# Attention with 77 keys: the softmax's exponentials taken head by head from the score bank, with bias and accumulated sum

## What is computed

```python
def _L0_xattn_ref(x, context, Wq, Wk, Wv, Wo, bo):
    scale = DIM_HEAD ** (-0.5)
    q = (x @ Wq).reshape(B, S, HEADS, DIM_HEAD).transpose(0, 2, 1, 3)
    k = (context @ Wk).reshape(B, L, HEADS, DIM_HEAD).transpose(0, 2, 1, 3)
    v = (context @ Wv).reshape(B, L, HEADS, DIM_HEAD).transpose(0, 2, 1, 3)
    attn = jnp.einsum('bhsd,bhld->bhsl', q, k) * scale
    attn = jax.nn.softmax(attn, axis=-1)
    out = jnp.einsum('bhsl,bhld->bhsd', attn, v)
    out = out.transpose(0, 2, 1, 3).reshape(B, S, INNER)
    return out @ Wo + bo

x = x + _L0_xattn_ref(_layernorm(x, axis=-1), ctx_768, ...)
x = x + _L0_ffn_ref(_layernorm(x, axis=-1), ...)
```

## Time and profile before

| | |
|---|---|
| median of 3 runs | 553.39 us (549.96 to 554.64) |
| the profiled execution | 549.97 us, its span 548.1 us |
| PE busy | 531.5 us, 97% of the span |
| DVE busy | 473.7 us, 86% |
| ACT busy | 294.8 us, 54% |
| POOL busy | 231.3 us, 42% |

### The profile page before, as it was taken

One profiled execution on the slowest core, in us unless ns is written; L12 is line 12 of the kernel. 1 busy time (PEld: TensorE's weight loads), 2 busy tenths in 40 slices (PEclk: granted clock), 3 DMA queues, 4 the chain that ended last, 5 costly groups with the idle time before them and its releaser, 6 DMA issues.

```text
span 548.1 us, 8031 instructions
## 1 busy us (share of the span) xinstructions
PE 531.5 (97%) x2704; PEld 357.9 (65%) x2704; DVE 473.7 (86%) x876; ACT 294.8 (54%) x414; POOL 231.3 (42%) x349
## 2 busy tenths in 40 slices
PE   8989889999999999999998799999999999999997
PEld 8868678887888878788777544444444445544444
DVE  4966888989989899898988599999999988899884
ACT  4834646556555654554443555555545533999500
POOL 4386749679596886856544000000000000055442
PEclk9999999999999999999999899999999999999999
DMA  8718365756668565435969917750442220399987
GB/s 310 277 45 304 104 187 180 249 181 192 209 206 252 171 224 185 154 101 182 202 99 329 269 33 293 273 145 24 117 115 46 70 39 15 121 327 229 149 107 129
DMA packets 82658, 93.82 MB, mean 171 GB/s; under 512 B 46801, under 2 KB 49873, under 8 KB 82361
## 3 DMA queue, kind: packets, MB, share of 16 engines
q1 hardware_dynamic: 77593, 84.13, 49.8%
q0 software_dynamic: 4320, 7.87, 9.6%
q10 hardware_dynamic: 704, 1.31, 0.8%
HBM read 47.51 MB, written 37.78 MB: 156 GB/s over the span
## 4 chain that ended last, share of the span: by engine, by line
PE 78%; DVE 11%; SPq 4%; DMA 2%; issue 2%; ACT 1%; POOL 0%; DVEq 0%; POOLq 0%
PE QO L1133 14%; PE SP L1133 14%; PE QO L193 5%; PE QO L195 5%; PE QO L194 5%; PE SP L464 4%; PE PTP L1240 3%; PE QO L1240 3%; PE SP L1240 3%; SPq L41 2%; SPq L37 2%; PE MI L584 2%; PE MI L583 2%; PE MI L582 2%; PE WOP L1240 2%
## 5 line engine op out<-in xcount | busy, mean ns | idle before, releaser
L45 POOL DMA_DIRECT2D out<-n2b x30 | 30.3, 1044 | 210.5 <-DVE n2b L1273 210.5
L1139 ACT ACTIVATE sil<-QO,fsc 128x512 f32<-128x512 f32 x88 | 60.5, 687 | 72.3 <-PE QO L1133 72.3
L1133 PE MATMUL QO<-nT,wgu 128*128 128x512 bf16 x352 | 90.3, 379 | 0.6 <-ACT nT L220 0.6
L1133 PE MATMUL SP<-nT,wgu 128*128 128x512 bf16 x352 | 90.3, 379 | 0.0
L1143 DVE SCALAR_TENSOR_TENSOR h<-SP,fsc,sil 128x512 f32<-128x512 f32 x88 | 65.9, 749 | 9.9 <-PE SP L1133 9.9
L505 POOL TENSOR_TENSOR PN<-P,rs 128x512 f32<-128x512 f32 x64 | 44.2, 712 | 50.3 <-DVE rs L497 50.3
L1146 DVE TENSOR_REDUCE hmx<-h 128x1 f32<-128x512 f32 x88 | 60.4, 686 | 3.0
L1133 PEld LDWEIGHTS QO<-nT,wgu 128*128 128x128 bf16 x352 | 34.4, 98 | 42.0 <-ACT nT L220 0.7
L1133 PEld LDWEIGHTS SP<-nT,wgu 128*128 128x128 bf16 x352 | 34.4, 98 | 41.5
L488 ACT ACTIVATE P<-P,r 128x616 f32<-128x616 f32 x32 | 26.0, 811 | 63.4 <-DVE P L484 63.4
L193 PE MATMUL QO<-xTs,wqs 128*128 128x512 f32 x124 | 50.4, 406 | 2.0 <-DVE xTs L224 1.7
(11 more groups left out here) (207 smaller groups left out, 1193.6 us busy)
## 6 DMA issues: line engine op xcount, KB each, us to landing
xTr<-in_xT SPq DMA_DIRECT2D x8, 1024.0 KB, 7.5
xn<-in_x SPq DMA_DIRECT2D x32, 256.0 KB, 3.9
out<-x SPq DMA_DIRECT2D x32, 256.0 KB, 2.9
n_rows<-n SPq DMA_DIRECT2D x32, 256.0 KB, 2.7
...
```

What stands on the lines that cost most here:

```text
L1133: m = e.matmul(ps, wv_[:, k, col:col + 128], nT[:, b % 2, :, k, :], start=(k == 0), stop=(k == 3))
L1139: t_sil[n] = add("act", lambda e: e.activation(sil[:, n % SR, :], gp, ACT.Silu, scale=fsc[:, ic:ic + 1]), [t_g[n], t_fs, t_h.get(n - SR)] ...
```

## The change

Per tile, the subtraction into P and the pass that sums P are left out. In their place VectorE makes a 128x8 tile `nb8`, minus the maximum times the scale column (`soft_shift`, in the place of `soft_sub`, and with its token `t_sub`), and the scalar engine takes eight exponentials, one for each head, straight from the score bank with `nb8`'s column as bias and the same scale column, each writing its 77 columns of P and the head's sum into `sm8`. All that waited for the subtraction as the last reader of the score bank now waits for the eighth exponential: the next S, `PV_rest`, and PT(30) for QO. The shift waits for `t_r8[n]` too, and the exponentials for the normalisation three tiles before (P) and the reciprocal two tiles before (`sm8`). Only the shift, not the exponentials, frees `mx8`.

```diff
@@ -114,6 +114,7 @@
         mx8 = sb(ctx, "mx8", [128, 2, H])
         sm8 = sb(ctx, "sm8", [128, 2, H])
         rs8 = sb(ctx, "rs8", [128, 2, H])
+        nb8 = sb(ctx, "nb8", [128, 2, H])
         clips = sb(ctx, "clips", [1, 2])
         sge = sb(ctx, "sge", [1, 2])
         sgp = sb(ctx, "sgp", [1, 2])
@@ -454,7 +455,7 @@
             if n == 30:
                 free = [t_oss[6, 0], t_oss[6, 1]]
             else:
-                free = [t_sub[29] if n == 31 else t_sub.get(n - 1)]
+                free = [t_exp[29] if n == 31 else t_exp.get(n - 1)]
             if t == 1 and b > 0:
                 free += [t_oss[b - 1, 2], t_oss[b - 1, 3]]
 
@@ -470,32 +471,31 @@
             return S_bank(n)[:, :].rearrange("p (a c) -> p a c", a=2)[:, :, 0:308].rearrange(
                 "p a (h l) -> p a h l", h=4)
 
-        t_mx, t_ag1, t_sum, t_rec = [Tokens() for _ in range(4)]
+        t_mx, t_ag1, t_rec = [Tokens() for _ in range(3)]
 
         def soft_max(n):
             mx = mx8[:, n % 2, :].rearrange("p (a h) -> p a h", a=2)
             t_mx[n] = add("dve", lambda e: e.reduce_max(mx, S4(n), AX.X), [t_S[n], t_sub.get(n - 2)],
                           "sm_max")
 
-        def soft_sub(n):
-            u = P[:, n % UR, 0:HL].rearrange("p (a h l) -> p a h l", a=2, h=4)
-            mb = mx8[:, n % 2, :].rearrange("p (a h) -> p a h", a=2).unsqueeze(3).broadcast_to(
-                [128, 2, 4, L])
-            t_sub[n] = add("dve", lambda e: e.tensor_tensor(u, S4(n), mb, ALU.subtract),
-                           [t_mx[n], t_norm.get(n - UR), t_wkl, t_ctxl], "sm_sub")
+        def soft_shift(n):
+
+            t_sub[n] = add("dve", lambda e: e.tensor_scalar(nb8[:, n % 2, :], mx8[:, n % 2, :], r8[:, n:n + 1], -1.0,
+                                                            ALU.mult, ALU.mult),
+                           [t_mx[n], t_r8[n], t_exp.get(n - 2)], "sm_sub")
 
         def soft_exp(n):
-            t_exp[n] = add("act", lambda e: e.activation(P[:, n % UR, 0:HL], P[:, n % UR, 0:HL], ACT.Exp,
-                                                         scale=r8[:, n:n + 1]),
-                           [t_sub[n], t_r8[n]], "sm_exp")
-
-        def soft_sum(n):
-            u = P[:, n % UR, 0:HL].rearrange("p (h l) -> p h l", h=H)
-            t_sum[n] = add("dve", lambda e: e.reduce_sum(sm8[:, n % 2, :], u, AX.X), [t_exp[n]], "sm_sum")
+
+            for hh in range(H):
+                at = (hh // 4) * 512 + (hh % 4) * L
+                t_exp[n] = add("act", lambda e, hh=hh, at=at: e.activation(
+                    P[:, n % UR, hh * L:hh * L + L], S_bank(n)[:, at:at + L], ACT.Exp, bias=nb8[:, n % 2, hh:hh + 1],
+                    scale=r8[:, n:n + 1], accum_out=sm8[:, n % 2, hh:hh + 1]),
+                               [t_sub[n], t_norm.get(n - UR), t_rec.get(n - 2), t_wkl, t_ctxl], "sm_exp")
 
         def soft_rec(n):
             t_rec[n] = add("dve", lambda e: e.reciprocal(rs8[:, n % 2, :], sm8[:, n % 2, :]),
-                           [t_sum[n], t_norm.get(n - 2)], "sm_rec")
+                           [t_exp[n], t_norm.get(n - 2)], "sm_rec")
 
         def soft_norm(n):
             u = P[:, n % UR, 0:HL].rearrange("p (h l) -> p h l", h=H)
@@ -510,7 +510,7 @@
             return QO if n == 30 else PTP
 
         def PT(n):
-            free = t_sub[30] if n == 30 else t_pl[29] if n == 31 else t_pl.get(n - 1)
+            free = t_exp[30] if n == 30 else t_pl[29] if n == 31 else t_pl.get(n - 1)
 
             def fn(e):
                 for k in range(5):
@@ -542,7 +542,7 @@
                 state["use"] += 1
                 banks.append((at, state["banks"][at], state["free"][at]))
             for k in range(2):
-                banks.append((None, SP[:, 512 * k:512 * k + 512], (t_sub[min(4 * b + 4, NT - 1)],)))
+                banks.append((None, SP[:, 512 * k:512 * k + 512], (t_exp[min(4 * b + 4, NT - 1)],)))
             pv_at[b] = banks
 
             def fn(e):
...
@@ -782,7 +781,7 @@
                 if s > 0:
                     S(s + 1)
                     soft_max(s + 1)
-                    soft_sub(s + 1)
+                    soft_shift(s + 1)
                 if 1 <= b < NB:
                     load_vb(b)
                 PT_high(s)
@@ -790,7 +789,6 @@
                     soft_exp(s + 1)
                 if t not in DEFER:
                     PT_low(s)
-                when("s", soft_sum, s + 1)
                 when("s", soft_rec, s + 1)
             elif t < 3:
                 if t == 1 and b + 1 < NB and s != 1:
@@ -799,11 +797,10 @@
                 when("s", soft_max, s + 1)
                 if late_low:
                     PT_low(s - 1)
-                when("s", soft_sub, s + 1)
+                when("s", soft_shift, s + 1)
                 when("s", soft_exp, s + 1)
                 when("am", largest, s - 7)
                 when("w", w_top, s - 1)
-                when("s", soft_sum, s + 1)
                 when("w", w_scale, s - 1)
                 when("s", soft_rec, s + 1)
                 when("w", w_inverse, s - 1)
...
@@ -938,32 +934,29 @@
             S(30)
             PT_high(28)
             soft_max(29)
-            soft_sub(29)
+            soft_shift(29)
             load_vb(7)
             load_wgu(2)
             load_wgu(3)
             soft_exp(29)
             soft_max(30)
-            soft_sub(30)
+            soft_shift(30)
             PT_low(28)
             soft_exp(30)
             normed(23)
-            soft_sum(29)
             soft_rec(29)
             soft_norm(29)
             wo(24)
             S(31)
-            soft_sum(30)
             soft_rec(30)
             soft_norm(30)
             soft_max(31)
-            soft_sub(31)
+            soft_shift(31)
             soft_exp(31)
             wo(25)
             residual(24)
             PT(29)
             PT_high(29)
-            soft_sum(31)
             soft_rec(31)
             soft_norm(31)
             PT_low(29)
```

8 lines of the change are left out of this document (3 added, 5 removed).

## The result

The changed kernel takes 593.37 us (median of three runs, 590.56 to 595.53) where the kernel before took 553.39: a ratio of 1.074, with an interval from 1.068 to 1.080. The profiled span grew from 548.1 to 593.7 us, by 45.6. The prediction said 579 us, with a range from 562 to 596: slower, as forecast, near the upper end of the range. By the medians 25.6 us of growth were forecast and 40.0 found; by the profiled spans, which the rest of this text uses, 27.3 and 45.6. The profiled execution is the slowest of the three (595.53 us, mean granted clock 0.967); the two others had spans of 591.5 and 588.7 us at clocks of 0.988 and 0.991. So some 5 us of what this profile shows come and go from one execution to the next, with the lowest clock in the longest one.

The account below looks back on a forecast made before the run. TensorE sets the pace, and the single score bank can delay it. Start 5.0, six batches 20.4 and last batch 1.9 sum to 27.3 us on 549.97, so 577.3; half the median's offset on top gives 579 us, range 562 to 596.

Parts of the forecast that it names:

- E: Scalar engine's block per tile, first exponential to last sum: 8 x 0.44 = 3.5 us, bounds 2.7 and 4.2.
- The first gap: Steady batch, first short interval between score products (3.84 us before): stall E - 1.2 = 2.3 us.
- The second gap: Steady batch, second short interval between score products (4.37 us before): stall E - 2.0 = 1.5 us.
- The 0.4 us returned per batch: Long gaps (9.8 us and more) give back 0.4 us, including TensorE's 0.28 us wait for a split of x.
- The start: S(1) to S(3): +2.9 at S(1), +1.5 between S(2) and S(3), 0.6 for the clock; +5.0 us.
- The last batch: Tiles 29 to 31 and the output projections behind them: +3.0 us, about 1.1 absorbed at the end, +1.9.
- The cheap block: Rival: a head costs 0.21 to 0.25 us with its sum, 552 to 557 us, no difference; chance 0.11.
- the faster kernel: Rival: VectorE's relief pulls in TensorE's waits, needing E below 1.2 us; 543 to 546 us; chance 0.03.
- The dearer block: Rival: sum a separate instruction draining the engine, 0.6 us a head; about 602 us; chance 0.18 shared with the clock.
- The clock rival: Rival: stalls lower TensorE's clock, 1.7 us each for six to twelve; 590 to 598; chance 0.18 shared with dearer block.
- is no bound: Scalar engine's load in the attention stage: gains 2.7 us per tile where it idles about 3.8 of 8.2 us.
- The signs: Profile after: 256 exponentials 0.34 to 0.53 us apart, S waiting twice a batch, VectorE 40 us less busy, batch 36 us.

Follow-up runs that it names:

- e4: Changed kernel with one maximum over all heads, one exponential of 616 columns per tile and VectorE's sum pass: 550.26 us, ratio 0.997 to the kernel before.
- e10: Changed kernel with four exponentials of 154 columns per tile, two heads sharing a maximum, and VectorE's sum pass: 557.16 us, ratio 1.010 to the kernel before.
- e5: Changed kernel without accumulated sums: eight exponentials from the score bank, the sum pass back on VectorE: 579.0 us, ratio 1.050 to the kernel before.
- e7: Changed kernel with matmuls of ones in TensorE's idle time and maxima in the score bank, so the shift reads PSUM: 581.24 us, ratio 1.054.
- e3: Changed kernel with matmuls of ones ahead of S(1), S(3) and S(4b+2), in TensorE's idle time: 589.18 us, ratio 1.069 to the kernel before.
- e6: Changed kernel with the maxima in eight unused columns of the score bank, so the shift reads PSUM: 583.68 us, ratio 1.059 to the kernel before.
- e2: Kernel before, VectorE's subtraction kept, its exponential cut into eight in place in SBUF with accumulated sums, no sum pass: 572.31 us, ratio 1.037.

## Why the prediction was right, and where it was short

**What bounds.** Right. TensorE set the pace, VectorE's relief was worth nothing (its busy time fell by 34.8 us, from 473.7 to 438.9, and the kernel got slower), and the loss came in through the one score bank, at the two short gaps. e4 and e10 fit the thresholds: at a block of 0.87 us neither gap stalls, at 1.59 the first does, by E - 1.2, and the second gains 0.08.

**The block.** E was put at 3.5 us, between 2.7 and 4.2; it is 3.3. The eight exponentials without the sum were put at 2.7, and take 2.56; the sum at 0.10 a head, and costs 0.09. The table that the prediction cites, in the Trainium skill's page "VectorE: DVE Perf Modes", section "The TRN2 errata — SBUF-src ops pay a fixed extra latency per instruction", gave an estimated 0.207 us a head. The rows of e5 show 0.305 between two starts, each with two column operands, and the measurement decides.

**The first gap.** 2.3 us forecast, 2.08 found in the changed kernel and with everything else undisturbed (e7): the step holds, with E = 3.3.

**The second gap.** "Stall E - 2.0 = 1.5 us", and 2.52 found: this step failed. Its mistake is the price of the shift, and that it left the clock out. The shift was priced by the reciprocal, an operation of the same size, as 0.20 us, with no question what GpSimd does at that moment. In e7, with the shift freed and the clock up, the gap is 5.79 us, so it has gained 1.42, which is the step's own number. The remaining 1.1 us, in five batches of six, belong to both delays, and either alone makes the gap nearly as long: the held-up shift alone 6.90 us (e3), the lower clock alone up to 6.69 (e6). In b = 1 the shift came just ahead of that addition (92.69 against 92.81) and took 0.23 us, the clock stayed up, and the gap is 5.80 us in the changed kernel too.

**The 0.4 us returned per batch.** Not returned: in e7 the two long gaps of b = 3 are 0.24 us longer together than before, not 0.4 shorter. TensorE's wait of 0.28 us for the split of x did go, but in its place it waits for a copy of q ahead of PV, in the changed kernel once in each of five batches:

```profile
155.38 0.50 PE L552 MATMUL QO<-pts,vbd 32*128 32x512 f32 x2 [0.60 <-ACT qs L221]
```

Over the six batches of e7 the long gaps grow by 2.3 us where 2.4 were counted as returned: 4.7 us of miss. The short gaps took back 1.8 of it (21.0 us where 22.8 were forecast), since the block is shorter than 3.5 us.

**The start.** 5.0 forecast, 11.9 found. S(1) was to move by 2.9 and moved by 3.7: its block starts 0.98 us late, since the shift of tile 0 stood 1.34 us behind GpSimd's splits. With the shift freed S(1) moves by 2.66 (e6). TensorE's idle time ahead of it became 5.67 us, and the clock behind it:

```profile
40.00:46.00 6.00, 4.71 (x14) 4.20 (x15) 1.93 (x4) 1.73 (x8) 1.38 (x2) 0.50 0.22 87
```

Six us at 0.50 for which I had added 0.6. With both edits (e7) the start costs 5.4, close to the 5.0, but partly by luck: S(1) moves by 2.4 (2.9 forecast), the gap from S(2) to S(3) grows by 1.9 (1.5 forecast), and 1.25 us lie between S(4) and S(5), where TensorE waits 2.52 us for a copy of q (0.89 before) and the lower clock follows. For that wait the prediction had no term. So what failed here is the shift's price, the clock's term and this copy of q; the chain to S(1) and S(3) held.

**The last batch.** 1.9 forecast, 2.5 in e7 for the last batch and what is behind it, 3.8 in the changed kernel. The 1.3 us between lie behind the last residual, in a stage that the prediction called unchanged: that residual stands 44.2 us later than before and the first product of the feed-forward 45.5. There the granted clock was 0.50 from 347 to 353 us; in the kernel before it was 0.50 from 304 to 307 and 0.98 from 307 to 310, at the same place of the program.

**The sum.** With the shift out of the way, and the clock but for one stretch in the start, e7 costs 5.4 + 23.2 + 2.5 = 31.1 us where the prediction has 5.0 + 20.4 + 1.9 = 27.3. The rest of the 45.6 us, 14.5, is what the shift and the clock do together. The result lies in the stated range because that was left wide for a dearer block and a milder case of the clock; neither came as it was priced, and to that extent the hit is luck. By the profiled spans e6 takes 11.8 us away by the shift alone and e3 5.7 by the clock alone; by the ratios (1.074, 1.059, 1.069) it is 8 and 2.5 us, since this profile of the changed kernel is one with a low clock.

**The rivals.** The cheap block and the faster kernel fell with E. The dearer block's condition held, since the sum is an instruction of its own, but not its price: a head takes 0.39 us and not 0.6. The clock rival was given 1.7 us for six to twelve stalls, and the text said that stalls of 2.3 us stay below what brings the clock down. That was wrong: 1.96 us of idle time were followed by 0.50 in the batch shown. But in the second gap a held-up shift hid it: filling TensorE's idle time gave the six batches nothing there (30.5 against 29.9 us), and 1.4 us once the shift was freed. The time lies in the clock rival's 590 to 598, by another road in good part.

**The load of the scalar engine.** That it "is no bound" came out nearly right for this kernel: TensorE's waits for copies of q come to 6.0 us there, 3.0 of them in the start. Most likely that is because the wait for the bank stretches the batch and so gives the scalar engine time, for e2 shows that with the bank's wait removed about half of the growth stays (24.5 of 45.6 us of span, 3.7 of 7.4%). The prediction's sum stood on a reason that is not the only one: by the load on that queue alone the kernel would have been slower by 3.7%.

**The signs.** The 256 exponentials are there, 0.39 us apart, and S waits for them twice a batch, 24.0 us in all where some 25 were named. The batch takes 37.6 us, not 36. VectorE's busy time fell by 34.8 us, not by 40 or more: the durations of the operations left out are 50.6 us and those of the shifts 11.4, which leaves 39.2, and neighbouring instructions overlap, so that the busy time falls by less than the durations.

**What stays open.** Why the same 1.96 us of idle time is followed by the lower clock in one batch or execution and not in another: in the changed kernel's profile it is in five batches of six, in that of e6 in two, and in e3 the 2.26 us ahead of 168.22 were followed by none, but the 2.28 ahead of 128.99 were. And how much of e2's 7.7 us in the start is the clock.
